# Keys and queries projected after the output projection, one place for the context's columns, two for the halves of q and k

## What is computed

```
query  = layernorm(x) @ w_q.T + b_q        # 16 heads of 32
key_   = ctx @ w_k.T + b_k
value  = ctx @ w_v.T + b_v
scores = where(causal, query . key_ / sqrt(32), -inf)
x = x + tanh(g_xattn) * (softmax(scores) @ value @ w_o.T + b_o)
xd, wd = fp6_blocks(layernorm(x)), fp6_blocks(w_f)
x = x + tanh(g_ffn) * (xd @ wd.T + b_f)
```

## Time and profile before

| | |
|---|---|
| median of three runs | 1390.96 us |
| profiled execution, device time | 1392.38 us |
| its span, first to last instruction | 1390.6 us |
| mean granted TensorE clock | 0.989 of full speed |
| first scores of batch 0 / of batch 31, in the span | 45.3 us / 1320.1 us |
| PE busy | 1354.2 us (97%) |
| DVE / POOL / ACT busy | 1124.7 / 938.7 / 916.6 us |

### The profile page before, as it was taken

How to read it: one execution, slowest core, us unless ns; L and a number is a source line. 1 busy time by engine, 2 the same in 40 slices (tenths; PEclk the granted TensorE clock), 3 DMA queues, 4 the chain that set the end, 5 groups by cost and what they waited for, 6 DMA issues and landing times.

```text
span 1390.6 us, 34895 instructions
## 1 busy us (share of the span) xinstructions
PE 1354.2 (97%) x10608; PEld 1198.5 (86%) x10608; DVE 1124.7 (81%) x4219; ACT 916.6 (66%) x2969; POOL 938.7 (68%) x1449
## 2 busy tenths in 40 slices
PE   7899999999999999999999999999999999999987
PEld 7788888898888888888888888888888889889865
DVE  5768888788888888888878878888888888888773
ACT  4667666667666666667666667666666666766661
POOL 1657776677676777676677676677677667767564
PEclk9999999999999999999999999999999999999998
DMA  8444344444444444434444434444444444443320
GB/s 253 118 112 107 103 111 124 118 129 107 109 109 120 124 128 117 107 101 119 121 126 123 108 99 115 126 119 124 110 106 109 126 118 128 110 116 99 88 62 31
DMA packets 181912, 159.10 MB, mean 114 GB/s; under 512 B 30176, under 2 KB 164320, under 8 KB 181728
## 3 DMA queue, kind: packets, MB, share of 16 engines
q1 hardware_dynamic: 181728, 156.88, 43.3%
HBM read 39.33 MB, written 16.78 MB: 40 GB/s over the span
## 4 chain that ended last, share of the span: by engine, by line
PE 59%; DVE 20%; SPq 9%; issue 5%; DMA 3%; ACT 1%; POOL 1%; DVEq 0%; ACTq 0%; POOLq 0%
PE proj L549 14%; PE proj L551 13%; PE proj L550 13%; SPq L380 9%; PE pT_ps L616 8%; DVE all_probs L891 5%; PE proj L632 3%; DMA k_stack<-k_lo 3%; DVE stats L899 3%; PE s_ps L605 3%; PE proj L660 2%; DVE all_probs L1028 2%; DVE k_lo L920 2%; PE s_ps L606 1%; DVE oT_lo L954 1%
## 5 line engine op out<-in xcount | busy, mean ns | idle before, releaser
L458 POOL TENSOR_TENSOR all_probs<-all_probs,rden 128x128 f32<-128x128 f32 (+1 forms) x1024 | 504.1, 514 | 347.5 <-DVE rden L949 346.5
L735 ACT ACTIVATE all_probs<-all_probs,neg_max 128x128 f32<-128x128 f32 (+1 forms) x1024 | 458.3, 449 | 242.4 <-DVE neg_max L891 242.2
L891 DVE CUSTOM_DVE_ANT_0 all_probs<-s_ps,causal 128x128 f32<-128x128 f32 (+1 forms) x1024 | 324.4, 354 | 144.2 <-PE s_ps L606 137.1
L616 PE MATMUL pT_ps<-ident,all_probs 128*128 128x128 f32 x1536 | 265.0, 282 | 9.9 <-POOL all_probs L458 7.2
L735 ACT ACTIVATION_READ_ACCUMULATOR all_probs<-all_probs,neg_max 128x1 f32 x1024 | 193.1, 189 | 0.0
L817 ACT ACTIVATE all_probs<-pT_ps 128x384 f32<-128x384 f32 x256 | 125.4, 490 | 87.4 <-PE pT_ps L616 87.2
L616 PEld LDWEIGHTS pT_ps<-ident,all_probs 128*128 128x128 f32 x1536 | 160.8, 142 | 25.2 <-issue 14.1
L549 PE MATMUL proj<-cT_hi,wk_hi 128*128 128x256 f32 x512 | 153.8, 300 | 1.4 <-DVE wk_lo L844 1.4
L605 PE MATMUL s_ps<-k_stack,q_stack 96*128 96x256 f32 x512 | 152.8, 299 | 2.1 <-DVE neg_max L891 2.0
L549 PE MATMUL proj<-aT_hi,wq_hi 128*128 128x256 f32 x512 | 151.0, 295 | 2.3 <-DVE aT_lo L943 2.3
L550 PE MATMUL proj<-cT_lo,wk_hi 128*128 128x256 f32 x512 | 142.7, 279 | 0.0
(11 more groups left out here) (119 smaller groups left out, 3607.9 us busy)
## 6 DMA issues: line engine op xcount, KB each, us to landing
k_stack<-k_hi SPq DMA_DIRECT2D x512, 64.0 KB, 2.0
q_stack<-q_hi SPq DMA_DIRECT2D x512, 64.0 KB, 2.1
xs_yz<-in_x SPq DMA_DIRECT2D x32, 512.0 KB, 5.2
k_stack<-k_lo SPq DMA_DIRECT2D x256, 64.0 KB, 2.0
q_stack<-q_lo SPq DMA_DIRECT2D x256, 64.0 KB, 2.1
out<-xs_yz SPq DMA_DIRECT2D x64, 256.0 KB, 2.3
c_quads<-in_ctx SPq DMA_DIRECT2D x124, 128.0 KB, 2.9
vs<-in_L_xattn_w_k SPq DMA_DIRECT2D x2, 512.0 KB, 5.8
```

What stands on the lines that cost most here:

```text
L458: last = nc.gpsimd.tensor_tensor(p, p, rden[:, sd, t, h:h + 1].to_broadcast([P, (1 + t) * P]), ALU.mult)
L616: last = nc.tensor.transpose(pT_ps[h % 2][:, m * P:(m + 1) * P], probs[:, h % P_RING, m * P:(m + 1) * P], ident[:, :])
L735: last = nc.scalar.activation(probs[:, h % P_RING, cols], probs[:, h % P_RING, cols], ACT.Exp, scale=-1.0, bias=neg_max[:, sd, t, h:h + 1] ...
L891: last = nc.vector.tensor_tensor_reduce(probs[:, h % P_RING, cols], s_ps[h % 2][:, cols], causal[:, (1 - t) * P:], 1.0, MASKED, ALU.add, A ...
```

## The change

The lists UNITS and SLOT_PARTS give way to one list of slots, SLOT_WORK, with a list of its own for step 1 and a table of lags. In a steady step the keys of half 0 go from slots 1 and 2 to slots 10 and 11 (behind o), the queries of half 0 from slots 9 and 10 to slot 12, and half 1 of v from slots 14 and 15 to slots 1 and 2 of the next step. cT_hi and cT_lo have one place in the place of two, and the context of a batch is turned one step later, in slots 3 and 5 (SP loads it later in the step). q_hi, q_lo, k_hi and k_lo get a place for each half, and ACT waits for the DMAs of the same half. SP loads x first in a step, and waits for the keys of half 0 before it stacks them. Both halves of xn are made in slot 1, and sixteen transposes of ident are put before the first weight's transposes. The number of matmuls, of DMAs and of their bytes in a steady step stays as it was.

```diff
-UNITS = [("q", 1, 2), ("dT", 0, 4), ("k", 0, 1), ("dT", 1, 4), ("f", 0, 4), ("xT", 0, 1), ("f", 1, 4), ("xT", 1, 1),
-         ("o", 0, 3), ("o", 1, 3), ("q", 0, 1), ("v", 0, 1), ("k", 1, 1), ("v", 1, 1)]
+LAGS = {("q", 0): 1, ("q", 1): 2, ("k", 0): 1, ("k", 1): 1, ("v", 0): 1, ("v", 1): 2, ("o", 0): 3, ("o", 1): 3,
+        ("f", 0): 4, ("f", 1): 4, ("dT", 0): 4, ("dT", 1): 4, ("xT", 0): 1, ("xT", 1): 1}
+SLOT_WORK = ("q1 q1 q1", "dT0 q1 v1", "v1 v1 v1", "dT1", "f0 f0 f0", "f0 f1 f1", "f1 f1", "xT0 xT1 o0 o0", "o0 o0 o1",
+             "o1 o1 o1", "k0 k0 k0", "k0", "q0 q0 q0 q0", "v0 v0 v0", "v0 k1 k1", "k1 k1")
+SLOT_WORK_1 = ("", "k0 k0 k0", "k0", "", "", "xT0", "xT1", "", "", "q0", "q0 q0 q0", "v0", "v0 v0 v0", "k1 k1 k1", "k1", "")
...
-WAKING = 12
+WAKING = (12, 16)
-SLOT_PARTS = (3, 3, 3, 1, 3, 4, 3, 3, 3, 3, 3, 1, 3, 3, 3, 2)
...
-XN_SLOTS = (1, 3)
+XN_SLOT = 1
-TURN_SLOTS = (5, 8)
-TURN_SLOTS_1 = (12, 13)
+TURN_SLOTS = (3, 5)
...
-        q_hi = sb("q_hi", [P, 2, S], F32R)
-        k_hi = sb("k_hi", [P, 2, S], F32R)
+        q_hi = sb("q_hi", [P, 2, 2, S], F32R)
+        k_hi = sb("k_hi", [P, 2, 2, S], F32R)
...
-                                     src[j * DK:(j + 1) * DK, :, :].bitcast(F32)).then_inc(
+                                     src[j * DK:(j + 1) * DK, pair, :, :].bitcast(F32)).then_inc(
...
             def step(i, ph):
+                if at(i, 0):
+                    load_first()
+                elif live(i):
+                    if i == 1:
+                        sp.wait_ge(done["cT"], 2)
+                        context(1)
...
+                    sp.wait_ge(x_in, 16 * i)
+                    sp.dma_start(xs[:, place(ph, 0), :, :], batch_of(x, i)).then_inc(x_in, 16)
                 if live(i - 2):
...
                     stack("k", i - 2, 1)
...
                     stack("q", i - 2, 1)
+                if i > 1 and live(i):
+                    sp.wait_ge(turned, 2 * (i - 1))
+                    context(i)
...
                         sp.wait_ge(max_ok, HEADS * (b - 1) + HEADS // 2)
-                    else:
-                        sp.wait_ge(left["k"], 2 * b + 1)
+                    sp.wait_ge(left["k"], 2 * b + 1)
                     stack("k", b, 0)
                     sp.wait_ge(left["q"], 2 * b + 1)
                     stack("q", b, 0)
...
             def transpose_weight(u, w, c):
+                if u == 0:
+                    for _ in range(WAKING[1]):
+                        nc.tensor.transpose(proj[BANKS - 1][:, 0:P], ident[:, :], ident[:, :])
...
-                    if some(n := b + half):
+                    if some(b):
                         for e in range(2):
-                            act.wait_ge(stacked[kind][1 - half][e], STACK_DMAS * 16 * n)
+                            act.wait_ge(stacked[kind][half][e], STACK_DMAS * 16 * b)
```

More of the change, by code:

```diff
@@ L99, in live, with units_of @@
         return not isinstance(b, int) or 0 <= b < B
[L101 to L104, removed]
+    def units_of(slot_work):
+        return [(s, (name[:-1], int(name[-1]))) for s, names in enumerate(slot_work) for name in names.split()]
+    assert all(sum(unit == u for _, u in units_of(SLOT_WORK)) == PARTS[unit[0]] for unit in LAGS)
     work = {}
@@ L111, in fused_kernel @@
             for s, (kind, half) in LAST_O:
-                work.setdefault((i, s), []).extend((kind, half, i - lag_of[kind, half], p) for p in range(PARTS[kind]))
+                work.setdefault((i, s), []).extend((kind, half, i - LAGS[kind, half], p) for p in range(PARTS[kind]))
         else:
[L114 to L117, removed]
+            part_of = dict.fromkeys(LAGS, 0)
+            for s, unit in units_of(SLOT_WORK_1 if i == 1 else SLOT_WORK):
+                if live(i - LAGS[unit]):
+                    work.setdefault((i, s), []).append((*unit, i - LAGS[unit], part_of[unit]))
+                part_of[unit] += 1
     work[1, 0] = [("cT", half, 0, 0) for half in range(T)] + work.get((1, 0), [])
@@ L318, in turn_slots @@
         def turn_slots(b):
-            return TURN_SLOTS_1 if b == 1 else TURN_SLOTS if b > 1 else ()
+            return TURN_SLOTS if b > 0 and live(b) else ()
         def finished(i, s, ago=1):
@@ L411, in step @@
                         sp.wait_ge(out_moved, 16 * T * (i - X_RING + 1))
+                    sp.wait_ge(x_in, 16 * i)
                     sp.dma_start(xs[:, place(ph, 0), :, :], batch_of(x, i)).then_inc(x_in, 16)
+                if live(i - 2):
+                    if some(n := HEADS * (i - 2)):
+                        sp.wait_ge(max_ok, n)
+                    sp.wait_ge(left["k"], 2 * (i - 2) + 2)
+                    stack("k", i - 2, 1)
                 if live(i - 2):
@@ L511, in step @@
                 for s in range(SLOTS):
-                    for t, turn_slot in enumerate(turn_slots(i)):
-                        if s == turn_slot + 2 and live(i):
-                            context_lo(i, t)
+                    for t, turn_slot in enumerate(turn_slots(i - 1)):
+                        if s == turn_slot + 2:
+                            context_lo(i - 1, t)
                     lag, h = (2, s - 1) if s else (3, SLOTS - 1)
@@ L541, in _ @@
             pe.wait_ge(ident_ok, 1)
-            for _ in range(WAKING):
+            for _ in range(WAKING[0]):
                 nc.tensor.transpose(proj[BANKS - 1][:, 0:P], ident[:, :], ident[:, :])
@@ L751, in unit @@
                 elif kind in ("q", "k"):
[L753 removed]
+                    if some(b):
                         for e in range(2):
[L755 removed]
+                            act.wait_ge(stacked[kind][half][e], STACK_DMAS * 16 * b)
                     dst, bias = (q_hi, bias_q) if kind == "q" else (k_hi, bias_k)
                     for m in range(2):
[L758 removed]
+                        last = nc.scalar.activation(dst[:, half, m, :], bank[:, m * S:(m + 1) * S], ACT.Identity,
                                                     bias=bias[:, 2 * half + m:2 * half + m + 1])
@@ L778, in context_hi @@
                 act.wait_ge(turned, 2 * (b - 1) + t + 1)
[L779 to L783, removed]
+                act.wait_ge(done["k"], 2 * b)
+                act.wait_ge(done["v"], 2 * b)
+                nc.scalar.activation(cT_hi[:, :, t * P:(t + 1) * P], cols[:, t, :, :],
                                      ACT.Copy).then_inc(hi_ok["cT"], 1)
@@ L820, in step @@
                         exponentials(i - 2, s, side(ph, 2))
-                    for t, turn_slot in enumerate(turn_slots(i)):
-                        if s == turn_slot + 1 and live(i):
-                            context_hi(i, t)
+                    for t, turn_slot in enumerate(turn_slots(i - 1)):
+                        if s == turn_slot + 1:
+                            context_hi(i - 1, t)
                     for chunk in weight_chunks(i, s - 1):
@@ L1028, in step @@
                         nc.vector.tensor_copy(probsT[:, h % AV_HEADS, :], pT_ps[0][:, 0:3 * P]).then_inc(pT_even, 1)
-                    if s in XN_SLOTS and i > 1 and live(i - 1):
-                        normal_rows(i - 1, XN_SLOTS.index(s))
+                    if s == XN_SLOT and i > 1 and live(i - 1):
+                        for t in range(T):
+                            normal_rows(i - 1, t)
                     for r in range(2):
@@ L1037, in step @@
                                 stage(of, half)
-                    for t, turn_slot in enumerate(turn_slots(i)):
-                        if s == turn_slot and live(i):
-                            turn(i, t)
+                    for t, turn_slot in enumerate(turn_slots(i - 1)):
+                        if s == turn_slot:
+                            turn(i - 1, t)
                     for chunk in weight_chunks(i, s - 1):
```

38 lines of the change are left out of this document (15 added, 23 removed).

## The result

The changed kernel takes **1618.05 us** (median of four runs, 1617.06 to 1624.2) against 1390.55 for the one before in the same comparison: a ratio of **1.164, 95% interval 1.161 to 1.168**. The profiled execution has a span of 1616.4 us and a mean granted clock of 0.926. The forecast was 1634 us, in a range of 1560 to 1685.

The account below looks back on a forecast made before the run. PE was taken to bound the loop, with SP's issue queue second. 1390.6 - 12 (wait gone) + 186 (stalls) + 68 (clock) = 1632.6, plus 1.8 around the span, gave 1634 us, range 1560 to 1685.

Parts of the forecast that it names:

- slot 12 starts, full clock: PE in a steady step: one part fewer ahead of slot 12, so it starts 30.6 us into the step.
- DVE's lag to k0's burst: DVE empties k0 in slot 12, 2.9 us after its start (2.1 to 3.4); SP can stack from 33.5 us.
- 17 issues: SP's queue: the sixth q0 DMA begins 17 x 0.67 = 11.4 us after k0's burst starts, at 44.9 us.
- stall: PE before head 0 of the next step: resumes at 47.0 us, not 40.96; 6.0 us a step, +186 us.
- clock behind it: PE after each stall: the granted clock falls, costing 2.2 us a step, +68 us (0 to 105).
- What bounds the kernel, and the wait that goes: The loop is PE-bound; ACT's 81.0 us wait to write k_hi goes with a second place: -12 us.
- SP's queue takes its place: SP waits for k0 behind slot 12, then 24 issues run on; one stall at slot 0, 31 times, +186 us.
- rival A: The clock holds behind each stall, all else as forecast without the +68: 1566 us, chance 0.15.
- The rest at nothing: v1's move, context's later turn and single place, both xn in slot 1, x load, waking transposes: taken as 0.
- Rival B: SP's stack issues cost 0.49 us with the gap: a 2.9 us stall, 1470 up to 1538 us, chance 0.05.
- C: SP's issue is no limit in the new place, or k0 comes out much earlier: 1379 us, chance 0.03.
- D: k1 or q1 miss head 8 as well, another 2 us a step: 1696 us, chance 0.06.

Follow-up runs that it names:

- fill: The changed kernel with 46 unread transposes of ident ahead of each batch's first scores from batch 1 on, filling PE's idle time: 1564.5 us.
- two_places: The kernel before with a place for each half of q and k alone; f's low weight part shares the high part's place: 1376.2 us.
- k_two_places: The kernel before with two places for k_hi and k_lo only, xn sharing the turned context's place, plus the sixteen waking transposes: 1373.4 us.
- k0_ahead: The changed kernel with k0 moved from slots 10 and 11 to 7 and 8, ahead of o, and the context turned in slots 3 and 4: 1440.2 us.
- k0_ahead_fine: The changed kernel with k0 in slots 7 and 8, a semaphore for each three stack DMAs, and dT0 last in slot 1: 1397.2 us.
- interleave: The changed kernel with SP's 24 issues alternating: six of k0, six of q0, second six of k0, second six of q0: 1562.1 us.
- q0_from_act: The changed kernel with q0's twelve DMAs issued by ACT in slots 14 and 15 in place of SP: 1552.2 us.
- before_wake: The kernel before with only sixteen transposes of ident added ahead of the first weight's: 1389.2 us.

## Why the prediction was right

By its own steps, for one step of the loop:

| term | forecast | measured |
|---|---|---|
| slot 12 starts, full clock | 30.6 | 30.7 (fill) |
| DVE's lag to k0's burst | 2.9 | 2.6 |
| 17 issues | 11.4 | 10.86 to 12.2, mean 11.3 |
| last issue to head 0 | 2.0 | 2.1 |
| stall | 6.0 | 5.6 (slot 15's 7.48 less 1.92) |
| clock behind it | 2.2 | 2.0 (slots 0 to 2); 1.8 by fill's whole step |
| step | 49.2 | 48.6 |

*What bounds the kernel, and the wait that goes.* Right, by both kernels with a second place: 40.97 us a step in place of 41.36, which is 12 us in 31 steps, as forecast. two_places was 14 us faster in all, k_two_places, with the waking, 17.

*SP's queue takes its place.* Right in mechanism and place: the burst starts behind slot 12, 24 issues follow without a pause, PE stops once a step ahead of head 0 and nowhere else, 31 times. k0_ahead moves k0 ahead of o, with the same 24 issues on the same queue, and the stall shrinks to 0.6 us. The stall was mis-sized by 0.4 us, most of it in DVE's lag: I went from slot 11's 2.6 us to 2.9 for the stages of o, but slot 11's 2.6 had such a stage ahead of it already. Rows 6 show those behind q_lo at 770.92; this one of the kernel before stands ahead of it:

```profile
769.83 0.55 DVE L966 TENSOR_SCALAR xs_yz<-xs_yz,mom,rstd 128x512 f32<-128x512 f32 x1
```

In 31 steps these 0.4 us are some 14 us, the largest part of the 16 between 1634 and 1618. That the total came no further off is in part luck: the clock (some 6 us) and the head (5.6) came out cheaper than forecast as well, and the last stretch (2.7) and the order of the slots (0.1 us a step) made up for some of it.

*The clock.* That it falls behind each stall was right, and rival A (1566 us) describes what fill shows by other means: 1564.5. The low stretches are 3.4 to 10.2 us long, 166 us of 1265 in the loop, but part of each lies in the idle time itself and costs nothing. At 2.0 us by the mean the term was 0.2 too large. The Trainium skill (TensorE: Matmul & The Clock Gate, section "HAM oscillation — how this bites in real kernels") says that with a DMA wait in every tile each tile starts with the slow clock. This trace agrees: the clock is 0.50 at the start of the step shown, low for a time in each of the 26 steps, and 0.93 over the loop.

*The rest at nothing.* The later turn, the single place and the two xn cost next to nothing in the loop: at full clock slots 0 to 14 take 39.18 us by the mean in fill and 39.05 in k_two_places. The head came out 5.6 us earlier in the profiled execution (39.7 us for batch 0's first scores). Four parts of v1 gone from step 1 would be 2.8 of it, the waking and the differences between executions the rest; they were not tried apart. The last stretch, from batch 31's first scores to the end, is 73.2 us in place of 70.5, as much as v1 is worth, which now falls there.

Rival B (cheaper issues) and C (no limit in SP) are out: the issue is 0.60 us in all of these kernels, wherever the burst stands. D is out too, the slack to head 8 was enough.

## What to carry to other kernels

A queue that is busy for 35 of 41 us is a second bottleneck, though no busy column shows it: count its issues, and lay them out in time against the moment from which they may start and the moment at which they are needed. Moving work to a later slot costs nothing on the engine that does it and may cost everything on the queue that carries its result. Here a buffer's second place alone was worth 1%, and with the reordering that came with it the kernel is 16% slower.

A stall that PE repeats is paid for twice, once as idle time and once in the clock behind it. Cover it with idle matmuls only if it can't be removed: fill recovered 54 us of 227, k0's earlier slots 178, and 221 with the finer waits and the later dT0 of k0_ahead_fine.

## What the runs showed that I had not expected

A stall that was split in two cost less clock. Over 26 steps, interleave's idle times of 1.5 and 2.7 us by the mean brought 65 us of low clock, q0_from_act's single ones of 3.9 us, less in total, 113 us, and the changed kernel's of 5.4 us 166. No run changed the split alone.

A DMA issued on ACT's queue takes no less time to issue than on SP's, 0.62 us against 0.60, and beside SP's stack it lands in 2.15 us against 2.0. A large load ahead of it matters more: in the changed kernel too, with one queue, the first stack DMA behind each 512 KB load of x lands in 3.9 us by the median, at least 3.6 in all 31, and the last ahead of it in 2.05.

Of the 1536 stack issues before, 77 took longer than 0.7 us, 1.27 us by the mean. In bursts that PE waits for they decide how one step differs from the next: the steps of the changed kernel lie between 47.7 and 49.9 us, those of k_two_places, where nothing waits for SP, all at 41.0.

In the first microseconds the granted clock is not to be read from its column. Over the first 18 us of the kernel before it reads 1.00, yet the first weight's eight transposes take 1.95 us there (rows 11) and 1.13 in before_wake:

```profile
0.00:18.00 18.00, 12.64 (x56) 11.59 (x57) 6.76 (x13) 5.68 (x10) 1.95 (x10) 1.00 0.87 258
```
